# The last pair of low parts in four units of attention: from VectorE to GpSimd

## The reference

```
h = x @ W + positional                        # 16 x 1024 x 128
h = h + attention0(layernorm(h))              # group norm, 8 heads of 64, 1024 x 1024 scores each
h = h + triangular_mlp(layernorm(h))
h = h + attention1(layernorm(h))              # 8 heads of 16, 1024 x 1024 scores each
h = h + switch_moe(layernorm(h))              # 16 experts, routed by the largest logit
# in both attentions: softmax(q k^T * scale) v
```

## Time and profile before

| | us |
|---|---|
| median of 3 runs | 6597.86 (6585.30 to 6608.09) |
| the profiled execution | 6587.05, of it span 6585.3 |
| TensorE matmuls busy | 5849.4 (89%), x40295 |
| DVE busy | 4245.7 (64%), x9610 |
| ACT busy | 3267.1 (50%), x6417 |
| GpSimd busy | 2719.6 (41%), x2471 |
| low-part pairs on GpSimd | 1822.5, x960 |
| mean granted TensorE clock | 0.934 of full speed |

### The profile page before, as it was taken

How to read it: one execution, slowest core, us unless ns; L and a number is a source line. 1 busy time by engine, 2 the same in 40 slices (tenths; PEclk the granted TensorE clock), 3 DMA queues, 4 the chain that set the end, 5 groups by cost and what they waited for, 6 DMA issues and landing times.

```text
span 6585.3 us, 128361 instructions
## 1 busy us (share of the span) xinstructions
PE 5849.4 (89%) x40295; PEld 4041.3 (61%) x40295; DVE 4245.7 (64%) x9610; ACT 3267.1 (50%) x6417; POOL 2719.6 (41%) x2471
## 2 busy tenths in 40 slices
PE   5889898998999989899898989989899898999985
PEld 3656665666666666666666656656666666666643
DVE  4466666666666666666666666666666666666653
ACT  2445555455555545555455555555555455555542
POOL 2534344443434434344443434434344443444411
PEclk7989999999999989999999999999999999999987
DMA  3222231322313223231222313223222222313212
GB/s 77 43 60 53 60 75 43 77 58 60 84 44 76 63 50 82 51 81 45 61 71 61 78 40 85 58 54 85 51 71 58 59 73 58 77 42 80 51 47 63
DMA packets 268146, 412.40 MB, mean 63 GB/s; under 512 B 41158, under 2 KB 198806, under 8 KB 257174
## 3 DMA queue, kind: packets, MB, share of 16 engines
q1 hardware_dynamic: 259222, 386.57, 24.7%
q0 software_dynamic: 8192, 16.79, 0.9%
HBM read 115.91 MB, written 78.12 MB: 29 GB/s over the span
## 4 chain that ended last, share of the span: by engine, by line
issue 45%; POOL 30%; PE 15%; DVE 6%; DMA 2%; SPq 1%; ACT 1%; POOLq 1%; DVEq 0%; ACTq 0%
POOL pr_lo L541 22%; PE bank L969 3%; POOL on L1360 3%; PE bank L997 2%; DVE mxh L1778 2%; POOL x_sort_d L1394 1%; POOL mx L1402 1%; PE bank L1035 1%; DMA stacks<-parts 1%; DVE z L1547 1%; PE bank L1020 1%; PE bank L1013 1%; PE bank L875 1%; POOL rs L1331 1%; PE bank L995 1%
## 5 line engine op out<-in xcount | busy, mean ns | idle before, releaser
L1778 DVE TENSOR_REDUCE mxh<-bank 128x1 f32<-128x512 f32 x4096 | 2776.1, 687 | 1713.2 <-PE bank L969 1688.3
L1236 ACT ACTIVATE pr<-bank 128x512 f32<-128x512 f32 x4096 | 2424.8, 597 | 2460.0 <-PE bank L997 2405.3
L969 PE MATMUL bank<-stacks 128*128 128x512 f32 x4096 | 2101.2, 514 | 486.9 <-DVE mxh L1778 372.9
L541 POOL TENSOR_TENSOR pr_lo<-pr 128x1024 bf16<-128x1024 f32 x960 | 1822.5, 1900 | 1027.1 <-ACT pr L1236 1026.9
L997 PE MATMUL bank<-stacks 65*128 65x512 f32 (+1 forms) x4096 | 1695.6, 414 | 12.0 <-DMA stacks<-mrow 6.7
L969 PEld LDWEIGHTS bank<-stacks 128*128 128x128 f32 x4096 | 814.8, 199 | 1255.4 <-DVE mxh L1778 966.1
L997 PEld LDWEIGHTS bank<-stacks 65*128 65x128 f32 (+1 forms) x4096 | 816.5, 199 | 177.9 <-ACT pr L1236 33.6
L1360 POOL TENSOR_TENSOR on<-on,o_r 128x128 f32<-128x128 f32 x512 | 234.5, 459 | 1669.2 <-DVE on L1808 1668.2
L995 PE MATMUL bank<-stacks 128*128 128x512 f32 x2048 | 842.1, 411 | 0.2 <-ACT pr L1236 0.2
L1020 PE MATMUL bank<-v,pr_lo 128*128 128x129 bf16 x8192 | 659.7, 222 | 6.5 <-POOL pr_lo L541 2.5
L1013 PE MATMUL bank<-v,pr 128*128 128x129 bf16 x8192 | 662.4, 224 | 0.8 <-ACT pr L1236 0.8
(11 more groups left out here) (192 smaller groups left out, 5706.4 us busy)
## 6 DMA issues: line engine op xcount, KB each, us to landing
stacks<-parts SPq DMA_DIRECT2D x384, 512.0 KB
stacks<-parts_d SPq DMA_DIRECT2D x224, 128.0 KB, 2.9
wring<-ew_d SPq DMA_DIRECT2D x384, 64.0 KB, 1.8
z<-x_sort_d SPq DMA_DIRECT2D x96, 256.0 KB, 3.3
y_sort_d<-z SPq DMA_DIRECT2D x96, 256.0 KB, 2.5
parts_d<-mx SPq DMA_DIRECT2D x16, 1024.0 KB, 4.5
stacks<-parts_d SPq DMA_DIRECT2D x224, 64.0 KB, 2.8
stage<-in_pe SPq DMA_DIRECT2D x16, 512.0 KB, 3.8
```

The lines of the kernel that those rows point to most:

```text
L541: return eng.tensor_tensor(low_of(u, kt - 1).rearrange("p a b -> p (a b)"), w, hi, ALU.subtract)
L969: mm(maxb[k % 2][:, :], qs[:, t * P:(t + 1) * P], ks[:, g * HALF:(g + 1) * HALF], start=True, stop=True).then_inc(max_filled.sem, 1)
L1236: act.activation(pr[:, at % 2, kt, :], score[k % 2][:, :], ACT.Exp, scale=SCALES[layer]).then_inc(exp_done.sem, 1)
L1778: dve.tensor_reduce(mxh[:, layer, n // 2, n % 2:n % 2 + 1], maxb[k % 2][:, :], AX_X, ALU.max)\
```

## The change

GpSimd now makes the fourth pair of every unit of layer 0, also of the first four. DVE's call and its semaphore lo_last are gone, and TensorE waits for lo_done alone, which counts four pairs for each unit.

```
-        lo_done = Counts(sem("lo_done"), LO_DONE[-1])
-        lo_last = Counts(sem("lo_last"), LEAD)
+        lo_done = Counts(sem("lo_done"), 16 * 4)
...
                 for kt in range(T):
-                    if j == 0 and kt == 6 and u < LEAD:
-                        te.wait_ge(lo_last.sem, lo_last.at(seg.l0, u + 1))
-                    elif j == 0 and kt % 2 == 0:
-                        te.wait_ge(lo_done.sem, lo_done.at(seg.l0, LO_DONE[u] + kt // 2 + 1))
+                    if j == 0 and kt % 2 == 0:
+                        te.wait_ge(lo_done.sem, lo_done.at(seg.l0, 4 * u + kt // 2 + 1))
...
                     if layer == 0 and kt in LO_STEPS:
                         lo_parts(pool, seg, at, kt - 1).then_inc(lo_done.sem, 1)
-                    elif kt == 0 and at > 0 and units_of(seg.kind)[at - 1][0] == 0 and units_of(seg.kind)[at - 1][1] >= LEAD:
+                    elif kt == 0 and at > 0 and units_of(seg.kind)[at - 1][0] == 0:
                         lo_parts(pool, seg, at - 1, T - 1).then_inc(lo_done.sem, 1)
...
                 for step, at, layer, u, kt in steps_of(seg.kind):
-                    if kt == 0 and at > 0 and units_of(seg.kind)[at - 1] in LEADING:
-                        lo_parts(dve, seg, at - 1, T - 1).then_inc(lo_last.sem, 1)
                     tiles_due(seg, step)
```

More of the change, by code:

```diff
@@ L1873 @@
 LO_STEPS = (2, 4, 6)
-LEADING = [(0, u) for u in range(LEAD)]
-LO_DONE = [3 * min(u, LEAD) + 4 * max(u - LEAD, 0) for u in range(17)]
 VALUE_STEPS = (2, 3, 5, 6)
```

## The result

| us | before | changed |
|---|---|---|
| median, first chip | 6602.27 (4 runs) | 6524.27 (4 runs, 6504.57 to 6527.85) |
| the profiled execution, of it span | 6587.05, 6585.3 | 6523.29, 6521.5 |
| median, second chip | 6689.01 (11 runs) | 6628.83 (5 runs) |
| median, third chip | 6693.74 (27 runs) | 6622.43 (4 runs) |

The change makes the kernel faster. The ratio on the first chip is 0.988, with an interval from 0.9852 to 0.9907: 78 us less, between 61 and 98. On the two others it is 0.991 (0.9895 to 0.9925), 60 us, and 0.9897 (0.9882 to 0.9912), 71 us. The two profiled executions of the first chip are 64 us apart, a pair on the third chip 62. I had forecast 43. The direction and the pauses came as worked out.

A forecast was written before the change was run, and what follows sets the result against it. TensorE's queue was taken as the bound. Pauses of 44 us and a clock term of -2 gave 42 to 43 us; 43 off the median 6597.86 made 6555 us, range 6528 to 6590.

The forecast's parts named there:

- What bounds the kernel: TensorE's queue sets the time, so its pauses count, unless a later pause takes them back; not GpSimd's low parts.
- Handover 0: Where unit (0,0) gives way to the next: TensorE's 1.00 us pause at L906 shrinks, gain 0.84 us a batch.
- Handover 1: Where unit (0,1) gives way: gain 0, as the wait for the third head's stack grows from 1.95 to about 3.0 us.
- Handover 2: Where unit (0,2) gives way: TensorE's pause of 3.22 us shrinks to 2.0, gain 1.22 us a batch.
- Handover 3: Where unit (0,3) gives way: 1.22 us earlier less a 0.43 us wait for GpSimd's late pair, gain 0.79 a batch.
- The sum of the pauses: All four handovers: 2.85 us a batch, 42.8 us for 15 batches, 44 with the first batch.
- The clock: TensorE's clock falls behind the stack wait (8 more, -14 us) and handover 2's pause (7 fewer, +12): net -2, bounds -15 and +22.
- Every stall is regained: Rival: the stack comes earlier, handover 1 gives 18 us more and 8 new clock falls don't come: about 6523; chance 8%.
- Late pair: Rival: pair 0.8 us later, handover 3 gives nothing, and handover 2's clock falls stay: 19 of 43 us remain, 6579; chance 15%.
- swallowed whole: Rival: another wait behind each handover takes back the whole gain, time 6598; chance 8%.
- GpSimd becomes the bound: Rival, at the four units in a row: GpSimd's added 121 us count and DVE's 78 go, 6641, slower; chance 7%.
- Theory F: Rival set up for the experiments: the 20 to 35 us beyond the forecast lie in the rest of the batch, outside the handovers.

## Why the prediction was off

*What bounds the kernel: right.* TensorE's pauses set the time. The chain's reading, by which GpSimd would have cost 43 us more, is refuted by 64 less.

*Handover 0: right.* 0.84 us a batch predicted, 0.82 to 0.85 measured.

*Handover 1: right.* Predicted was nothing, the wait for the stack growing to 3.0; it is 2.82 to 3.10, and moving this pair alone gains nothing. The argument from two batches that reached the stack at the same time after the handover held.

*Handover 2: right, by its parts.* The pair starts 0.36 us behind the normalization, as worked out; the scale is there 3.50 after it (predicted 3.59). The pause is 2.10 where I said 2.0, so 1.12 us are gained and not 1.22. L1544 was held, as I had feared, by 0.6 us, and nobody waited for it.

*Handover 3: right.* 0.79 predicted, 0.77 measured. The pair starts 0.35 behind the normalization and TensorE waits for it; the row has 0.19 for it where I had 0.43, which changes nothing, since the end of the pair sets the matmul's start in both.

*The sum of the pauses: right,* 43 predicted and 41 measured.

*The clock: wrong, and this is the step that failed.* I took "the wait for the stack grows to 3.0 (8 more falls, -14 us), the pause at handover 2 shrinks to 2.0 (7 fewer, +12)", net -2. The second half is right: 7 to 9 fewer, in each of the three profiles of the changed kernel. The first is not: at 3.0 us there were 4, 7 and 5 falls, where at 2.0 there had been 6 and 7. The three and one falls behind handover 1's stall went as well. So there are 10 to 12 fewer falls and not 1 more. Their price has to be taken from the low-clock time, since a fall at the stack lasted up to twice as long in the changed kernel: 26 us less of it, or 11 to 12 us gained at the handovers where I had a loss of 2. With the pauses that makes 53 of the 62 and 64 us between the profiles, and of the medians' 60, 71 and 78.

Where did the 8 come from? I had read the frequency at one place, 3.2 us at handover 2, as a property of a pause of that length. The table of the grid says otherwise: what goes with a fall is where the pause ends, and 63 of the 70 long pauses at handover 2 ended where nearly every pause is followed by a fall. Moving the end of handover 2's pause by 1.12 us moved it on the grid too. The Trainium skill (TensorE: Matmul & The Clock Gate, What's actually happening) says that the watching of the engine's activity runs freely and is not started by the kernel, so that the same work can meet it at another phase. The traces agree: three profiles of one kernel have 4, 7 and 5 falls at one pause, and the place on the grid divides the falls from the rest in all but 2 of the 199 pauses of the table's first three rows. What length does by itself at one place on the grid is not shown, and neither is why the changed kernel's waits end so often in the middle part.

*My bound for the clock, +22 us, would have held this,* with 13 fewer falls. I left the likeliest value at -2 and centred the range on it; the time of the first chip lies 4 us below its low end. Some 15 of the 78 us there are beyond the profiles' 64, and fit the profiled execution of the kernel before having been 15 under its median. By the ratios of the two other chips the time would have been 6543 and 6534, inside the range: the miss of the range is a near one, that of the clock's sign is not.

*Rivals.* "Every stall is regained" gives about the measured time, 6523, by the wrong way: its 18 us from handover 1 did not come, as moving that pair alone shows; its other half, that the 8 new falls would not come, did. "Late pair", "swallowed whole" and "GpSimd becomes the bound" are refuted by the waits of 0.19 at handover 3 and by the time. Theory F, gains in the rest of the batch, has a share that stays open: on the first chip the rest of the batches is 14 us shorter with no edit there, on the third 6. The low-clock time there was 543 and 573 us in the two profiles of the kernel before, and 488, 539 and 526 in the three of the changed kernel. Whether the change brings that about, or how the batches happened to fall, no run here decides. I had put nothing for it.

*Two rules.* By the figure of 2 times of the Trainium skill (GPSIMD Engine Reference, Engine selection) the forecast had a variant with a gain of 35 us; the pairs take 1895 ns against DVE's 1215, 1.56 times, also when they are 1024, and the variant falls. What the same page of the Trainium skill says on the shared SBUF interfaces (Key points) the trace bears out once more: L1544 takes 1.73 us over a GpSimd pair where it took 1.13, and L1357's mean falls from 459 to 403 ns with DVE's pairs gone. Of L1772's executions, in the kernel before, 27 took over 1.5 us, and all 27 lay over a GpSimd pair; of the 100 that took under 0.4 us, 13 did.

## What to carry to other kernels

Work that is slower on the engine it moves to can still be faster, if it leaves the engine that frees the bottleneck's buffers; price it by the pauses at each place, and look in the trace for a batch that was already late or early to see which of them a later wait takes back. A pause costs its own length and then what the clock loses behind it, which at the handovers was 12 of 53 us: count the low-clock time at each place, look where the pauses end on the grid of the clock's changes, and give the term a range that is centred on no assumption from another place. Work on constants in a pause is worth its place only if it can start when the pause starts and leaves little of it.

## What the runs showed of the hardware

Filling pauses with matmuls on constants, with nothing taken away, made the kernel before 26 us and the changed one 23 to 45 us faster. The clock fell behind none of the pauses cut to about 1.3 us (fourteen in one kernel, ten in another), and behind four of the five of 2.8 to 2.9 us in the second. Of the same pause of 2.1 us at handover 2, 3 to 6 of 15 had a fall; it fell when the pause ended less than 0.53 or more than 1.76 us after a point of the grid (25 of 25) and never when it ended between (0 of 45).

A GpSimd instruction of 0.40 us took 1.31 beside DVE's pair and 0.40 at the same place with the pair gone.

The kernel before took 6602 us on one chip and 6689 to 6694 on three others, at a mean granted clock of 0.934 in the profile of the first and 0.931 in that of one other. The ratio of the changed kernel carried from chip to chip within 0.3% (0.988, 0.991, 0.9897), the time did not.
